# One softmax tile in four normalised by VectorE, steps of the attention reordered, dequantisation of the second weights begun earlier

## What is computed

```python
# x: (16, 128, 1024) f32, ctx: (16, 128, 256) f32
u = layernorm(x)                                  # over the last axis
q = Wq @ u; k = Wk @ ctx; v = Wv @ ctx            # Wq, Wk, Wv, Wskip: 128 x 128, per batch
att = softmax(q.T @ k / sqrt(128), axis=-1)       # (1024, 256) per batch
x = x + Wskip @ u + (att @ v.T).T
y = layernorm(x)
g = y @ Wg.T; h = y @ Wu.T                        # Wg, Wu dequantised, 2752 x 1024
x = x + (silu(g) * h) @ Wd.T                      # Wd dequantised, 1024 x 2752
```

## Time and profile before

| | |
|---|---|
| median of 3 runs | 1409.62 us (1408.81 to 1410.72) |
| the profiled execution | 1410.51 us, of which 1408.4 us from first to last instruction |
| TensorE busy | 98% (6414 matmuls) |
| VectorE, ScalarE, GpSimd busy | 79%, 49%, 22% |
| line 583, FFN products | 796.1 us |
| steps of attention | from 11 to 217 us |
| first FFN product | starts at 205.6 us, within the last steps of attention |
| mean granted TensorE clock | 0.997 |

### The profile page before, as it was taken

The page is one execution under the profiler, slowest core; times in us unless marked ns, Lnnn a source line. Parts: engine busy times, 40 slices in busy tenths (PEclk is TensorE's granted clock), DMA queues, the critical chain, the costliest instruction groups (busy, mean ns, idle before and its releaser), DMA issues.

```text
span 1408.4 us, 19596 instructions
## 1 busy us (share of the span) xinstructions
PE 1386.9 (98%) x6414; PEld 679.2 (48%) x6414; DVE 1117.2 (79%) x1597; ACT 690.1 (49%) x1279; POOL 310.2 (22%) x365
## 2 busy tenths in 40 slices
PE   8999998999999999999999999999999999999999
PEld 6766764444444444444444444444444444444443
DVE  5898978887877878778788788788788788788476
ACT  6899994344344444444444444444444444434430
POOL 1132332122122222122212212222212212212200
PEclk9999999999999999999999999999999999999999
DMA  5422222286576576576666756746746746747696
GB/s 160 132 90 96 86 90 61 53 152 120 102 136 125 105 137 117 103 138 112 122 123 117 132 112 114 147 94 123 137 104 122 126 104 119 134 97 151 114 295 262
DMA packets 58982, 174.83 MB, mean 124 GB/s; under 512 B 8000, under 2 KB 11072, under 8 KB 54592
## 3 DMA queue, kind: packets, MB, share of 16 engines
q0 software_dynamic: 34560, 83.90, 38.5%
q1 hardware_dynamic: 24096, 90.20, 20.5%
q10 hardware_dynamic: 288, 0.26, 0.1%
HBM read 73.67 MB, written 100.66 MB: 124 GB/s over the span
## 4 chain that ended last, share of the span: by engine, by line
PE 92%; DVE 3%; ACT 2%; issue 1%; DMA 0%; POOL 0%; SPq 0%; DVEq 0%; POOLq 0%; ACTq 0%
PE ps L583 52%; PE ps L621 9%; PE ps L623 9%; PE ps L622 9%; PE ps L549 3%; PE ps L521 3%; PE ps L786 2%; PE ps L509 2%; PE ps L544 2%; PE ps L745 1%; PE ps L538 1%; ACT temps L849 1%; ACT temps L823 1%; DVE neg_max L1276 0%; PE ps L499 0%
## 5 line engine op out<-in xcount | busy, mean ns | idle before, releaser
L583 PE MATMUL ps<-xt,w_gu 128*128 128x512 f16 x3528 | 796.1, 379 | 5.7 <-DVE temps L1492 1.7
L583 PEld LDWEIGHTS ps<-xt,w_gu 128*128 128x128 f16 x3528 | 344.9, 98 | 422.6 <-ACT temps L929 2.6
L962 ACT ACTIVATE stage<-ps,pow 128x512 f32<-128x512 f32 x300 | 204.3, 687 | 321.4 <-PE ps L623 315.9
L1522 DVE SCALAR_TENSOR_TENSOR stage<-ps,pow,stage 128x512 f32<-128x512 f32 x220 | 160.2, 747 | 105.2 <-ACT stage L962 68.0
L621 PE MATMUL ps<-park 128*128 128x512 f16 x560 | 212.3, 379 | 1.5 <-ACT stage L962 1.5
L622 PE MATMUL ps<-park 128*128 128x512 f16 x560 | 212.2, 379 | 0.0
L623 PE MATMUL ps<-park 128*128 128x512 f16 x560 | 212.2, 379 | 0.0
L435 POOL DMA_DIRECT2D out<-stage x80 | 70.6, 883 | 428.5 <-DVE stage L1522 428.5
L449 POOL DMA_DIRECT2D out<-stage x80 | 69.2, 865 | 294.4 <-ACT stage L962 294.4
L959 ACT CAST park<-temps 128x512 f16<-128x512 f32 x140 | 83.2, 615 | 64.8 <-DVE temps L1506 38.1
L1519 DVE TENSOR_TENSOR park<-temps,park 128x512 bf16<-128x512 f32 x140 | 98.4, 709 | 17.0 <-ACT park L959 14.0
(11 more groups left out here) (135 smaller groups left out, 1625.2 us busy)
## 6 DMA issues: line engine op xcount, KB each, us to landing
out<-stage POOLq DMA_DIRECT2D x80, 512.0 KB, 5.3
out<-stage POOLq DMA_DIRECT2D x140, 256.0 KB, 5.5
grid<-grids SPq DMA_DIRECT2D x136, 256.0 KB, 6.0
raw<-packed SPq DMA_DIRECT2D x34, 512.0 KB, 4.3
out<-stage SPq DMA_DIRECT2D x16, 512.0 KB, 2.7
stage<-x SPq DMA_DIRECT2D x12, 512.0 KB, 3.5
xt<-out SPq DMA_DIRECT2D x12, 512.0 KB, 11.9
out<-xt SPq DMA_DIRECT2D x12, 512.0 KB, 2.6
```

The source lines that it names most:

```text
L583: mm = pe.matmul(bank, w_gu[e][:, wp, w, P * j:P * j + P], xt[:, xb, xp, j, cols], start=(fresh and n == 0), stop=(n == 3 * J - 1), skip_g ...
L962: return act.activation(dst, ps[:, bank, :], ACT.Copy, scale=pow2[:, 10:11])
L1522: return dve.scalar_tensor_tensor(out=part, in0=ps[:, bank, :], scalar=pow2[:, 10:11], in1=part, op0=ALU.mult, op1=ALU.add)
```

## The change

It does six things.

1. `normalize_probs` on ScalarE handles three of the four tiles; the fourth is multiplied by VectorE within `inverse_total`, right behind the reciprocal, for which VectorE waits on its own semaphore. TensorE waits for both before it transposes.
2. The first maxima (batch 0, half 0) are taken in two reductions of two tiles; ScalarE's first two exponentials wait for the first reduction only.
3. TensorE issues the energies of batch 1, half 0, at the end of step 0, ahead of the values and transposes there; ScalarE makes keys 1 right after the first exponentials.
4. In every step ScalarE does `exponentials(i, 0)` ahead of a `sum_hi`, and `values_out` ahead of the other; VectorE does `normalize(1, i-2)` ahead of the block, and `add_attention(i-1, 0)` ahead of `inverse_total(i, 0)`.
5. Job 0 of the weights is packed into earlier steps (to step 12, where it was to step 14), with ScalarE's roundings at the ends of steps 8 and 11 (from 9 and 13); job 1's nibbles, subtractions and scales take steps 14, 15 and 16, and the first FFN tile has each of the rest one gap earlier.
6. SyncE issues the loads of job 1 after the store of batch 10, ahead of the last load of x.

```diff
--- before.py
+++ after.py
@@ -223,11 +223,14 @@
         s_xn = sem("s_xn")
         s_xn2 = sem("s_xn2")
         s_mixed = sem("s_mixed")
+        s_first_energy = sem("s_first_energy")
+        s_first_max = sem("s_first_max")
         s_energy = sem("s_energy")
         s_max = sem("s_max")
         s_exp = sem("s_exp")
         s_inv = sem("s_inv")
         s_prob = sem("s_prob")
+        s_prob3 = sem("s_prob3")
         s_prob_t = sem("s_prob_t")
         s_prob_t_sb = sem("s_prob_t_sb")
         s_att = sem("s_att")
@@ -343,9 +346,10 @@
                     load_grid(0, 0)
                 if i >= 4:
                     store_batch(i - 4)
+                if i == B - 2:
+                    load_grid(1, 2)
+                    load_raw(1, 4)
             store_batch(B - 4)
-            load_grid(1, 2)
-            load_raw(1, 4)
             for i in range(B - 3, B):
                 store_batch(i)
             with sp.Fori(2, 3 * PAIRS + 2, 1) as j:
@@ -502,6 +506,7 @@
 
             def probs_transposed(b, f):
                 pe.wait_ge(s_prob, 2 * b + f + 1)
+                pe.wait_ge(s_prob3, 2 * b + f + 1)
                 for h in range(2):
                     bank_free(("probs", b, f, h))
                     bank = ring_bank(("probs", b, f, h))
@@ -519,6 +524,8 @@
                 for t in range(NTH):
                     cols = slice(P * (NTH * f + t), P * (NTH * f + t) + P)
                     mm = pe.matmul(ps_e[f][:, t, :], xn[b % XNS][:, cols], kk[:, par, :], start=True, stop=True)
+                    if b == 0 and f == 0 and t == 1:
+                        mm.then_inc(s_first_energy, 1)
                 mm.then_inc(s_energy, 1)
 
             def block_transposed(unit):
@@ -559,7 +566,8 @@
             keys_values(0)
 
             for i in range(B):
-                energies(i, 0)
+                if i != 1:
+                    energies(i, 0)
                 if block_of_step(i, "between"):
                     block_transposed(block_of_step(i, "between"))
                 if i >= 1:
@@ -571,6 +579,8 @@
                     keys_values(i + 1)
                 if block_of_step(i, "after"):
                     block_transposed(block_of_step(i, "after"))
+                if i == 0:
+                    energies(1, 0)
                 if i >= 1:
                     values(i - 1, 1)
                 probs_transposed(i, 0)
@@ -818,8 +828,11 @@
                     act.copy(prob_t[:, f, h, :], ring_bank(("probs", b, f, h))).then_inc(s_prob_t_sb, 1)
 
             def exponentials(b, f):
-                act.wait_ge(s_max, 2 * b + f + 1)
+                if b or f:
+                    act.wait_ge(s_max, 2 * b + f + 1)
                 for t in range(NTH):
+                    if b == 0 and f == 0 and t % 2 == 0:
+                        act.wait_ge((s_first_max, s_max)[t // 2], 1)
                     ex = act.activation(prob[:, NTH * f + t, :], ps_e[f][:, t, :], ACT.Exp,
                                         bias=neg_max[:, f, t:t + 1], accum_out=total[:, f, t:t + 1])
                 ex.then_inc(s_exp, 1)
@@ -843,8 +856,9 @@
                          mixed(k, u).rearrange("p (j h) r -> p j h r", h=2)).then_inc(s_sum_hi, 1)
 
             def normalize_probs(b, f):
+
                 act.wait_ge(s_inv, 2 * b + f + 1)
-                for t in range(NTH):
+                for t in range(NTH - 1):
                     pr = prob[:, NTH * f + t, :]
                     pn = act.activation(pr, pr, ACT.Copy, scale=inv_total[:, f, t:t + 1])
                 pn.then_inc(s_prob, 1)
@@ -853,28 +867,28 @@
                 k = (i - 3) // 2
                 if block_of_step(i, "between"):
                     block_hi(block_of_step(i, "between"))
+                if i < B:
+                    exponentials(i, 0)
+                if i == 0:
+                    keys_out(1)
                 if k >= 1:
                     sum_hi(k - 1, T1 if i % 2 else T4)
-                if i < B:
-                    exponentials(i, 0)
                 if i < B:
                     normalize_probs(i, 0)
                 if i >= 1:
                     probs_out(i - 1, 1)
-                if i == 0:
-                    keys_out(1)
                 if i < B:
                     exponentials(i, 1)
                 if block_of_step(i, "after"):
                     block_hi(block_of_step(i, "after"))
                 if 0 < i < B - 1:
                     keys_out(i + 1)
+                if i + 1 < B:
+                    values_out(i + 1)
                 if i % 2 == 0 and k >= 0:
                     sum_hi(k, T3)
                 elif k >= 1:
                     sum_hi(k - 1, T2)
-                if i + 1 < B:
-                    values_out(i + 1)
                 if i < B:
                     probs_out(i, 0)
                 if i < B:
@@ -917,9 +931,9 @@
             values_out(0)
             for i in range(STEPS):
                 step(i)
-                if i == 9:
+                if i == 8:
                     plain_hi(0, 0)
-                elif i == 13:
+                elif i == 11:
                     mixed_hi(0, 0, 0)
                     mixed_hi(0, 0, 1)
 
@@ -1060,7 +1074,7 @@
                 if 1 <= at < 5:
                     block_hi(LATE[at - 1])
                     sum_hi(*((LAST - 1, T1), (LAST - 1, T2), (LAST - 1, T4), (LAST, T3))[at - 1])
-                if at == 2:
+                if at == 1:
                     plain_hi(2, 1)
                 if at == 4:
                     mixed_hi(4, 1, 0)
@@ -1272,6 +1286,14 @@
                     dve.wait_ge(s_x_in[i % 2], 16 * (i // 2 + i % 2))
 
             def maxima(b, f):
+                if b == 0 and f == 0:
+                    dve.wait_ge(s_first_energy, 1)
+                    dve.tensor_reduce(neg_max[:, 0, 0:2], ps_e[0][:, 0:2, :], X_AXIS, ALU.max, negate=True
+                                      ).then_inc(s_first_max, 1)
+                    dve.wait_ge(s_energy, 1)
+                    dve.tensor_reduce(neg_max[:, 0, 2:4], ps_e[0][:, 2:4, :], X_AXIS, ALU.max, negate=True
+                                      ).then_inc(s_max, 1)
+                    return
                 dve.wait_ge(s_energy, 2 * b + f + 1)
                 dve.tensor_reduce(neg_max[:, f, :], ps_e[f], X_AXIS, ALU.max, negate=True).then_inc(s_max, 1)
 
@@ -1316,18 +1338,21 @@
             def inverse_total(b, f):
                 dve.wait_ge(s_exp, 2 * b + f + 1)
                 dve.reciprocal(inv_total[:, f, :], total[:, f, :]).then_inc(s_inv, 1)
+                dve.wait_ge(s_inv, 2 * b + f + 1)
+                pr = prob[:, NTH * f + 3, :]
+                dve.tensor_scalar(pr, pr, inv_total[:, f, 3:4], None, ALU.mult).then_inc(s_prob3, 1)
 
             def step(i, meanwhile=None):
                 if i < B:
                     maxima(i, 0)
+                if i >= 2:
+                    normalize(1, i - 2)
                 if block_of_step(i, "between"):
                     block_done(block_of_step(i, "between"))
-                if i >= 2:
-                    normalize(1, i - 2)
+                if i >= 1:
+                    add_attention(i - 1, 0)
                 if i < B:
                     inverse_total(i, 0)
-                if i >= 1:
-                    add_attention(i - 1, 0)
                 if 1 <= i and i + 1 < B:
                     normalize(0, i + 1)
                 if 0 < i < B:
@@ -1452,22 +1477,25 @@
                 dve.wait_ge(s_grid_in, 16 * QG)
                 minus_zero((q_int, r_int)[nib], nib + 1)
 
-            def second_job():
-                job_nibbles(1)
-                job_minus(1)
+            def all_of(*parts):
+                def work():
+                    for part in parts:
+                        part()
+                return work
 
             first_job = {
                 2: powers_of_two,
                 4: first_raw,
                 5: lambda: first_minus(0),
-                6: lambda: first_minus(1),
-                7: lambda: times_scale(q, 1, 6),
-                8: lambda: times_scale(r, 2, 6),
-                11: lambda: plain_lo(0, 0),
-                12: lambda: first_sums(0, 0),
-                13: lambda: second_sums(0),
-                14: lambda: mixed_lo(0, 0),
-                16: second_job,
+                6: all_of(lambda: first_minus(1), lambda: times_scale(q, 1, 6)),
+                7: lambda: times_scale(r, 2, 6),
+                9: lambda: plain_lo(0, 0),
+                10: lambda: first_sums(0, 0),
+                11: lambda: second_sums(0),
+                12: lambda: mixed_lo(0, 0),
+                14: lambda: job_nibbles(1),
+                15: lambda: job_minus(1),
+                16: lambda: job_scale(1, 6),
             }
 
             step(0, extremes)
@@ -1644,13 +1672,12 @@
                     normalize(1, B - 1)
                     block_done(LATE[0])
                 if at == 2:
-                    job_scale(1, 6)
```

(4 more changed lines are left out.)

## The result

The changed kernel takes 1418.06 us (median of 6 runs, 1417.16 to 1420.35) against 1409.57 before (median of 6): ratio 1.0062, 95% interval 1.0052 to 1.0072. That is 8.5 us more. The forecast was 5.6 us less, and the time lies above the whole range.

What follows compares the result with a forecast made beforehand. TensorE was taken as the bound almost end to end, with ScalarE and VectorE nearly full. Start 3.0, holes 2.3, VectorE's lag -1.8 and first FFN tile 2.1 gave 5.6 us: 1404.0 against 1409.6, range 1402.5 to 1406.

Steps and rivals of the forecast that it cites:

- The start: First steps: earlier maxima and energies bring batch 2's energies to 28.3 us from 31.34, a gain of 3.0 us.
- the clock fall at 15.0: At the start, TensorE's clock was assumed to fall at 15.0 us as it did before; energies then end at 17.5.
- from there TensorE is the last again in both kernels: After batch 2's energies near 28 us, TensorE bounds both kernels, so the 3.0 us lead stays.
- VectorE's tile: Attention steps: two more tiles a step on VectorE, 0.32 us each; its lag costs TensorE 1.8 us, bounds 0 and 4.9.
- that pause: In each attention step, TensorE's small wait for `values_out` stays, since its copy waits for TensorE's own product; no change.
- the rival of GpSimd: Steps 4 to 15: GpSimd holds up 24 new VectorE tiles, 0.25 us each, 6 us more, 1414.6 us; chance 8%.
- ScalarE's holes: Three TensorE waits for late ScalarE copies close as ScalarE loses one tile in four: gain 2.3 us, bounds 0.8 and 2.3.
- The first FFN tile: First FFN tile: rests and sums come earlier on VectorE, shortening TensorE's waits by 2.1 us, bounds 1 and 3.
- SyncE's queue: Last x and ctx load some 3 us later, at about 167 us, but are used near 176; cost 0.
- The change touches nothing after some 270 us: The rest of the program after attention and the first FFN part was taken as unaffected, with no term.

Runs made afterwards that it cites:

- e8: Kernel before with only the split first maxima, batch 1's energies in step 0 and keys 1 behind the first exponentials: 1407.08 us, ratio 0.9991.
- e10: Kernel before with only VectorE's new order of steps: 1414.85 us, ratio 1.0040.
- e5: Changed kernel with VectorE's old order and all four tiles back on ScalarE: 1406.89 us, ratio 0.9987.
- e1: Changed kernel with VectorE's old order of steps, the fourth tile still on VectorE: 1413.89 us, ratio 1.0033.
- e2: Changed kernel with the fourth tile back on ScalarE, all else kept: 1413.37 us, ratio 1.0032.
- e6: Changed kernel with VectorE's old order, job 0's loads one batch later, four added ScalarE waits a step, 95 VectorE memsets behind the loop: 1409.88 us.
- e3: Changed kernel with the loads of job 0 issued one batch later: 1417.34 us, ratio 1.0051.
- e4: Kernel before with only the fourth tile moved to VectorE, orders untouched: 1413.91 us, ratio 1.0034.
- e9: Kernel before with the reworked start and the fourth tile on VectorE in only four halves, around steps 10 and 14: 1409.94 us, ratio 1.0003.
- e11: Kernel before with the reworked start, four tiles on VectorE, job 1's new packing and earlier loads, and the first FFN tile's rests and sums earlier: 1407.98 us.
- e7: Kernel before with 32 one-column memsets on VectorE, one behind each reciprocal: 1410.56 us, ratio 1.0012.

## Why the prediction was wrong

**The start: nearly right in size, wrong in what gives it.** Energies of batch 1 at 14.5 forecast, 14.10 measured; those of batch 2 at 28.3 forecast, 27.77 measured; 3.0 against 3.6 us. I let the clock fall at 15.0 as before. It didn't: 1.00 from 13 us on in after and e8. And e10 has 2.9 us of this lead with the old program of the start: in its execution the idle stretch before 16.27 was 2.67 us and not 3.67, and the clock stayed up. So most of the gain is the clock that doesn't fall, and only some 0.4 us (28.43 against 28.02 in e8) the reordered work. More runs bear this out, though a mean doesn't say where the clock fell: over the whole run it is 1.000 in 9 of 10 executions of e8, with a median of 1407.05 us, and in only 10 of the 76 of before that stand beside the experiments, and those 10 have a median of 1407.5. The sentence "from there TensorE is the last again in both kernels" failed: GpSimd's reduction, which I had in no row, took 3.0 of the 3.6 away by batch 3 (34.21 for 31.63), and with what follows 4.1 us by batch 4. The early loads alone don't do it: e5 and e8 issue the first of job 0 at 25.0 us, as early as after (24.7), and GpSimd goes on at 30.7. In these single executions it is later where VectorE's new order or its tile is there too (after 34.2, e1 34.3, e2 32.7) than in e5 with neither; but e6, which has the tile and later loads, has 31.7. Later loads brought 1.1 us in e3, about what chance gives, and 2.6 in e6 against e1, where more was changed. What in the machine slows the reduction stays open.

**VectorE's tile: its length right, its price in the right range by luck.** 0.32 us estimated, 0.35 measured (0.39 in the mean of after, 0.353 in e1). I charged 1.8 us for the lag, with 0 and 4.9 as bounds; it is 1.7 in after (e2) and 3.3 on the kernel before (e4). But in after the 1.7 are lost before batch 4, with GpSimd, and in all the steps that I priced the tile costs nothing (e5). On the kernel before it costs in steps 5, 7, 9, 10, 13 and 14, where I had steps 6, 7, 12 and 13 with their jobs, and through maxima, exponentials and `values_out`. ScalarE's new order, in which `values_out` comes earlier, may be what makes the tile free in after; it wasn't tried alone. I had named that pause and put it at no change, "its copy waits for TensorE's own product". It waits for that only while VectorE is ahead.

**The new order of VectorE: no term at all.** This is the step that failed most: the sum 3.0 + 2.3 - 1.8 + 2.1 has nothing for it. I costed part 4 on ScalarE (0.5 us for `sum_hi`) and on VectorE by its load alone, and moving work doesn't change a load. The path was to be read from the order: the reciprocal is what ScalarE waits for, and behind the change the second layernorm, a block and `add_attention` stand ahead of it. It costs 6.7 us on the kernel before (e10), and 4.7 in after from batch 4 to the first FFN product (e1). Part of it is the rival of GpSimd, in another place: I had priced the 0.83 us of the earlier trace rows for the new tiles, with a chance of 8%; the tiles are hardly held (0.39 for 0.35), but line 1281, moved beside GpSimd's operation, is held by the full 0.83 us in odd steps: 9 of its 32 executions in after are above 1.2 us, and 2 of 32 in before (I had seen one). The Trainium skill, GPSIMD Engine Reference, Key points, has the shared interfaces that I cited; the traces agree with it, in every odd step from the fifth on (1.63 us each in after).

**ScalarE's holes: closed, and worth little.** The waits of steps 10 and 14 are gone in after, shrunk to 0 and 0.46 in e9, as forecast. In after that isn't the tile's doing alone: in e5, with all tiles on ScalarE, they are gone too, and stand at 123.7 (0.63) and 162.2 us (1.06), behind the steps 8 and 11 to which the roundings were moved. The +2.3 us were not had, since on the kernel before the same tiles open waits of 0.7 us (e4, e9), and four of them brought 0.2. Closing a hole was costed without asking what comes due 4 us later. The page that I weighed, Perfetto Trace Analysis, Optimizing Scalar/DVE Operations, of the Trainium skill, says that moving work off VectorE may make sense when it is saturated. The move the other way, onto VectorE at 89%, lost 3.3 us on the kernel before (e4), and nothing from batch 4 on in after (e2, e5): the load alone doesn't tell.

**The first FFN tile: right.** 2.1 forecast, 1.85 measured in after, 1.86 in e5, 1.88 in e11. The wait of 1.3 is gone, that of 1.7 fell to 1.26 and not to 0.9. The jobs packed earlier, or ScalarE's new order, which no run has apart from them, cost something on the way there: e5 is 1.6 us behind e8 at the first FFN product, and has five waits for ScalarE's copies where e8 has three.

**SyncE's queue: right at 0.** No wait for the last x or ctx shows in after.

**"The change touches nothing after some 270 us": wrong.** It touches no instruction there, but it makes ScalarE's stream shorter and VectorE's longer, by one instruction for each half. The stall of 3.9 us that ScalarE had at the loop's end (1.5 us of TensorE) goes to the last stage, and one of 3.1 us on VectorE joins it: -1.7 and +4.4 us, 2.7 of the 7.7. That it is the fetching of instructions is my reading: the queue of DMA that is named for them has 20 packets of 8 KB in after and 19 before, each of the 20 such rows of ScalarE and VectorE of 2.8 us or more in these thirteen traces has the start of such a packet within it, and lengths alone bring a stall to the last stage (e7) and take both from it (e6). Most such packets, those of the attention among them, have no stall beside them. Shown is that length moves the stalls. Those of the last stage lie where the DMA moves 284 GB/s (1360 to 1416 us in after), those at the loop's end where it moves 144 (1300 to 1360), against 123 from 300 to 1360; whether the load there makes them long wasn't tried.

The sum as measured on the traces: start -3.6, its loss by batch 4 +4.1, the steps from there +6.3 (order 4.7, ScalarE's order and the earlier jobs 1.6, tile 0), first FFN tile -1.9, loop's end -1.7, last stage +4.4, together +7.7 (with rounding).

## What to carry to other kernels

When an order is changed on an engine that isn't the bound, its load says nothing: list for each result that another engine waits for what now stands ahead of it, and beside whose work each operation now runs. An idle stretch closed by moving work to a nearly full engine can open another one, so follow the moved work to the next result that is due. And look at the whole span after any change in the number of instructions: the same edit can be worth 3 us more or less far behind it.

## What the runs showed of the hardware

- A 128x1024 f32 multiplication-and-subtraction by per-partition values on VectorE took 0.81 us, and 1.64 while GpSimd ran a 128x512 operation of two inputs of 1.16 us: it began with GpSimd's and its excess is 0.83.
- ScalarE and VectorE stood 2.8 to 4.6 us waiting for nothing that the program waits for, mostly once each in an execution, all of them at the end of the loop and in the last stage; 32 one-column memsets of 0.06 us, placed in the first 200 us, cost 1.7 us at 1389.
- TensorE's clock fell to 1.2 GHz at idle stretches of 3.67 us (before), 2.57 (e3), 2.56 (e1), 2.55 (e9) and 2.17 (e6), and did not at 2.67 (e10), 2.56 (after) and 2.1 (e11). Those of after, e1 and e3 stand at the same place of the same instructions. So the length of the stretch alone does not decide; what else does stays open. A fall cost 1.7 us in e6, and 2.9 at the start, there together with the longer idle stretch.
- GpSimd's reduction over partitions has a record of 0.4 to 0.8 us in the profile, from 23.2 to 24.1 us on, and GpSimd's next operation comes only at 30.7 to 34.3 us, with nothing missing for it that the profile names. Two kernels that are alike up to there (e8, e9) differ by 0.95 us in this.
